# Prologue of an adaptive feed-forward kernel on one core: the adapters' split, the variances' norm and the value product take other places around tile 0

## The chip, the cores and the metric

The kernel runs on one core of one Trainium2 chip. The metric is the device time of one execution in microseconds (us), the median of several runs. A core has five engines that run their own instruction streams and wait for each other with semaphores: TensorE (PE: matmuls, with its weight loads shown apart as PEld), VectorE (DVE), ScalarE (ACT), GpSimd (POOL) and SyncE (SP), which here issues nearly all DMAs.

## The reference

The input x holds 128 samples of 64 channels by 1024 values. Cut to what matters:

```python
def layer0(x):                        # cond: one 64x64 matrix per sample, picked from 16
    h = einsum('bct,bcd->bdt', x, W0[itok_B_0_15])
    query = h @ Wq.T                                        # 64 wide
    scores = (query @ Wr.T) @ (aux_keys @ Wr.T).T / sqrt(48) + log_rel     # 256 slots
    top 8 of scores -> softmax(query . key / 8 + log_rel) -> weighted sum of aux_values
    aux_out = that @ Wvd.T @ Wvu.T
    log_var = log1p(var(h)); norm_var = log_var / (mean(log_var) + 1e-6)   # mean over all rows
    learned = gelu(h @ Wu1.T + bu1) @ Wu2.T + bu2
    gate = sigmoid(.5 * clip((clip(.5*norm_var + 2.5*sigmoid(learned), 0, 5) - .5) / 1.5, 0, 1) - 1)
    return h + gate * aux_out         # gate under 0.05 is 0
def layer1(x):                        # cond: base weight plus a rank-16 adapter, one of 32 per sample
    y = x @ base_weight.T + base_bias + (x @ A[ids].T) @ B[ids].T
    return y @ W_base.T + b_base + fourier_update(y)        # linear in y
x = x + layer0(x);  x = x + layer1(x)
```

All of the second layer is linear, so the kernel folds it into one 1024x1024 matrix M and one constant row. `norm_var` needs the mean over all 8192 rows before any tile can be gated.

## The kernel before, in words

The 128 samples form 64 tiles of two samples: 128 rows by 1024 columns. The program has three stages, whose parts for each engine run one after the other on it.

- `setup_stage` and `fold_stage` build M (`m32`, eight chunks of 128x1024) and the adapters' right side, and compute every tile's row variances beside it.
- `main_stage` has a prologue and then `step(n, p)` for n = 0 to 64. Step n takes tile n through its first products and finishes tile n - 1. Step 0 stands alone in the code and carries prologue work beside it; the steps behind it run in a loop of two steps a turn. Within each engine the order of instructions is exactly the order in which the code is written; nothing is rescheduled.

Matmuls in high precision are split in a high and a low part and done as three products (`product3`, lines 81 to 85). The low part of M, `m16_lo`, is made one chunk at a time on DVE by `m_low(k)` (line 1402) from `m32` and the high part that ACT made in `m_high(k)`.

Step 0 on each engine, as far as the change touches it:

- PE: tile 0's first product with 24 matmuls (lines 83 to 85), then the product with the picked matrices (line 1323), for which it waits for `pa_lo` from DVE (line 1535). Then the mean of the variances (line 1331) and the big product with M, eight chunks of six matmuls (line 1346). Chunk k waits for `m_low(k)` (line 1338). Between chunks stand, behind chunk 1, a transposition of the query (line 1355, waits for `wa_ready`, because it overwrites the bank in which the adapters' product lies); behind chunk 3 the router's scores (lines 1367 and 1368, which wait for the transposed query and for `norm_ready`, since they overwrite the bank of the mean); behind chunk 5 `value_operand()` (line 1253, waits for `vb_ready`, since it overwrites the bank that `v_low` reads); behind chunk 6 the transpositions of the softmax weights (line 1375, wait for `exp_ready`). At the end PE waits for `vd_ready` (line 1380).
- DVE: prologue work up to `gates` (line 1475), `m_low(1)`, `m_low(2)`, then step 0 with `pa_lo` (line 1535), the query's two halves (lines 1541, 1543) and `z` (line 1545). Then `beside_first()`: `m_low(3)`, the adapters' split `wa_split` (lines 1489, 1490), `m_low(4)` to `m_low(7)`, `v_low` twice (line 1482, the low part of the value projection, two copies), the four small instructions of the norm (lines 1499 to 1502). After it the rest of the step: `arg` (line 1551), MAX8 (line 1555) on the scores and the top-8 chain, softmax and gate down to `scale` (line 1597), and the copy `vd` (line 1601).
- ACT: step 0's part, among it `m_high(4)` to `m_high(7)`, the copy `rhs_a` of the value projection (line 1109), the splitting of x for tile 1, the exponential (line 1147).
- POOL: the low parts of x for tile 1: `a_raw` (line 1178), `xt_lo` (line 1179), `x16_lo` (line 1184).
- SP: stores `wa_split` to memory (line 1000) after `wa_ready`, then waits for that store and for `vb_ready`, and loads the adapters of tiles 0 and 1 (lines 942 and 950; eight DMAs a tile), which the end of step 1 needs (line 1290).

Of the kernel before, what the change touches and what calls it, by code (L numbers as in the profile page):

```python
# [37 lines left out]
ALU = mybir.AluOpType  # L38
# [6 lines left out]
KC = HID // P  # L45
HALF = HID // 2
NCOND = 16
NLORA, RANK = 32, 16
# [22 lines left out]
def f(ap):  # L71

    return ap.bitcast(F32)
# [7 lines left out]
def product3(pe, out, a_hi, a_lo, b_hi, b_lo, start, stop, skip=False):  # L81

    pe.matmul(out, a_hi, b_hi, start=start, stop=False, skip_group_check=skip)  # L83
    pe.matmul(out, a_hi, b_lo, start=False, stop=False, skip_group_check=skip)  # L84
    return pe.matmul(out, a_lo, b_hi, start=False, stop=stop, skip_group_check=skip)  # L85
# [10 lines left out]
def known_positive(count):  # L96

    return not isinstance(count, int) or count > 0
# [676 lines left out]
def main_stage(nc, t, g, v, f_, pair, sem, tile, st):  # L775
# [88 lines left out]
    misc_ps = pair[3][:, HALF:HID]  # L864
# [6 lines left out]
    wa_split = b["pm_lo"][:].rearrange("p (l s r) -> p l s r", s=2, r=RANK)  # L871
# [21 lines left out]
    s = {n: sem("m_" + n) for n in names}  # L893
# [142 lines left out]
    def has_new(n):  # L1036
        return not isinstance(n, int) or n < NT

    def has_old(n):
        return not isinstance(n, int) or n > 0  # L1040

    def arrived(n, p, each):

        return (n - p) * (each // 2) + each
# [152 lines left out]
    def tensor(pe):  # L1197
# [49 lines left out]
        def value_operand():  # L1247

            pe.wait_ge(s["av_in"], 32)
            pe.wait_ge(s["vb_ready"], 1)  # L1250
            for c in range(2):
                for k in range(KC):
                    last = pe.matmul(out_ps[:, c * BOT:(c + 1) * BOT], av_t[:, k, c * P:(c + 1) * P],
                                     b["wvd_t"][:, k, :], start=(k == 0), stop=(k == KC - 1))
            last.then_inc(s["vd_mm_done"], 1)
# [4 lines left out]
        def step(n, p):  # L1260
# [56 lines left out]
            if has_new(n):  # L1317

                pe.wait_ge(loaded["bd"][p], arrived(n, p, BPT))
                pe.wait_ge(s["pa_lo_ready"], n + 1)  # L1320
                if known_positive(n):
                    pe.wait_ge(s["z_ready"], n)
                product3(pe, mix_ps[:, 0:HQW], b["bd"][:, p, 0, :], b["bd"][:, p, 1, :],
                         b["pa_hi"][:, p, HQ[p]], b["pa_lo"][:, p, HQ[p]],
                         True, True).then_inc(s["mixq_done"], 1)
                if known_positive(n):
                    pe.wait_ge(s["pm_lo1_ready"], n)
                if not has_old(n):
                    pe.wait_ge(s["lsum1_ready"], 1)
                    pe.wait_ge(s["router_split"], 2)  # L1330
                    pe.matmul(score_ps[:, 0:1], g["ones"][:], b["mean"][:, 0:1], start=True, stop=True
                              ).then_inc(s["mean_done"], 1)
                    pe.wait_ge(s["const_placed"], 17)
                pe.wait_ge(s["x16_lo_ready"], n + 1)
                for k in range(KC):
                    if not has_old(n):
                        pe.wait_ge(s["m16_hi_ready"], k + 1)
                        pe.wait_ge(s["m16_lo_ready"], k + 1)
                    x_h = b["x16_hi"][:, p, k * P:(k + 1) * P]
                    x_l = b["x16_lo"][:, p, k * P:(k + 1) * P]  # L1340
                    first, end = k == 0, k == KC - 1
                    for lhs, m, a, z in ((x_h, m16_hi, first, False), (x_h, m16_lo, False, False),
                                         (x_l, m16_hi, False, end)):
                        for h in range(2):
                            c = slice(h * HALF, (h + 1) * HALF)
                            last = pe.matmul(pm_ps[:, c], lhs, m[:, k, c], start=a, stop=z)  # L1346
                    if end:
                        last.then_inc(s["s1b_done"], 1)
                    if k == (0 if has_old(n) else 1):
                        pe.wait_ge(s["q_split"], n + 1)  # L1350
                        if not has_old(n):
                            pe.wait_ge(s["wa_ready"], 1)
                        if known_positive(n):
                            pe.wait_ge(s["hm_ready"], n)
                        pe.transpose(misc_ps[:, 0:P], f(b["query"][:]), g["ident"][:]
                                     ).then_inc(s["qt_done"], 1)
                    if k == (2 if has_old(n) else 3):

                        pe.wait_ge(s["qt_ready"], n + 1)
                        if not has_old(n):  # L1360
                            pe.wait_ge(s["norm_ready"], 1)
                        if known_positive(n):
                            pe.wait_ge(s["logits_ready"], n)
                        if not has_old(n):
                            pe.wait_ge(s["logrel_placed"], 64)
                            pe.wait_ge(s["router_split"], 2)
                        pe.matmul(score_ps, b["q_a"][:], b["router_a"][:], start=True, stop=False)  # L1367
                        pe.matmul(score_ps, b["q_b"][0:BOT + 2, :], b["router_b"][0:BOT + 2, :],  # L1368
                                  start=False, stop=True).then_inc(s["score_done"], 1)
                    if k == 5 and not has_old(n):  # L1370
                        value_operand()
                    if k == 6:
                        pe.wait_ge(s["exp_ready"], n + 1)
                        for c in range(2):
                            last = pe.transpose(misc_ps[:, (c + 1) * P:(c + 2) * P],  # L1375
                                                b["probs"][:, c * P:(c + 1) * P], g["ident"][:])
                        last.then_inc(s["et_done"], 1)

                if not has_old(n):
                    pe.wait_ge(s["vd_ready"], 1)  # L1380

        steps(pe, step)

    def vector(dve):
# [3 lines left out]
        def link(ins):  # L1388

            chain[0] += 1  # L1390
            ins.then_inc(s["m_chain"], 1)
            dve.wait_ge(s["m_chain"], chain[0])
# [7 lines left out]
        def m_low(k):  # L1400
            dve.wait_ge(s["m16_hi_ready"], k + 1)
            dve.scalar_tensor_tensor(m16_lo[:, k, :], m32[:, k, :], M_SCALE, m16_hi[:, k, :],
                                     ALU.mult, ALU.subtract).then_inc(s["m16_lo_ready"], 1)
# [71 lines left out]
        dve.tensor_scalar(b["gates"][:, 3:6], b["gates"][:, 0:3], 0.5, None, ALU.mult  # L1475
                          ).then_inc(s["gates_ready"], 1)

        m_low(1)
        m_low(2)

        def v_low(p):
            return dve.tensor_tensor(b["rhs_b"][0:BOT, p, :], out_ps[0:BOT, :], f(b["rhs_a"][0:BOT, :]), ALU.subtract)

        def beside_first():

            m_low(3)
            dve.wait_ge(s["wa_mm_done"], KC // 2)
            wa3 = misc_ps.rearrange("p (l r) -> p l r", r=RANK)
            link(dve.tensor_copy(wa_split[:, :, 0, :], wa3))
            dve.tensor_tensor(wa_split[:, :, 1, :], wa3, f(wa_split[:, :, 0, :]), ALU.subtract  # L1490
                              ).then_inc(s["wa_ready"], 1)
            for k in range(4, KC):
                dve.wait_ge(s["v_mm_ready"], 1)
                m_low(k)
            dve.wait_ge(s["va_ready"], 1)
            v_low(0)
            v_low(1).then_inc(s["vb_ready"], 1)
            dve.wait_ge(s["mean_done"], 1)
            link(dve.tensor_scalar(b["mean"][:, 1:2], score_ps[:, 0:1], 1.0 / (NT * P), 1e-6, ALU.mult, ALU.add))
            link(dve.reciprocal(b["mean"][:, 2:3], b["mean"][:, 1:2]))  # L1500
            link(dve.tensor_scalar(b["lv_num"][:], b["lv_log"][:], b["mean"][:, 2:3], 0.5, ALU.mult, ALU.mult))
            dve.tensor_scalar(g["norm_var"][:], b["lv_num"][:], 1.25, None, ALU.add
                              ).then_inc(s["norm_ready"], 1)

        def step(n, p):
            if has_old(n):
# [26 lines left out]
            if has_new(n):  # L1533
# [13 lines left out]
                if not has_old(n):  # L1547
                    beside_first()
# [146 lines left out]
```

## Time and profile before

| what | value |
|---|---|
| median of 3 runs | 1592.76 us (1592.39 to 1595.8) |
| profiled execution, its own time | 1595.65 us |
| its span, first to last instruction | 1593.8 us |
| PE busy | 1549.6 us, 97% of the span |
| DVE, ACT, POOL busy | 55%, 52%, 32% |
| chain that ended last, by engine | PE 85%, POOL 6%, issue 5% |
| PE, longest wait in the stretch from 300 to 345 us | 9.3 us, in front of line 1367 |

Times in the rows are microseconds from the span's start, unless marked ns. A row of the timeline gives start, duration, engine, line, operation, output and inputs; in brackets stands how long the engine had been idle before it, and what released it. "issue" as a releaser means that the profile found no instruction whose end fits. Consecutive instructions of one engine overlap a little, since one starts while the last drains, so the distance of two starts is what an instruction costs its queue.

### The profile page before, as it was taken

What the parts mean: (1) busy time and instruction counts of PE and PEld (TensorE: products, weight loads), DVE (VectorE), ACT (ScalarE), POOL (GpSimd) and SP (SyncE); (2) the same over time, 40 slices, a digit from 0 to 9 for tenths busy, and PEclk for the clock granted to TensorE, in tenths of its full rate; (3) what the DMA queues carried; (4) which work ended last, traced back from release to release, by engine and by line L of the source; (5) the groups of instructions that cost most, each with busy time, mean ns of one, the idle gap of its engine ahead of it and who ended that gap; (6) DMA issues with size and microseconds to landing.
All of it is one profiled execution on the core that took longest, in us unless ns stands there. A gap on an engine that the chain in (4) does not pass through costs nothing.

```text
span 1593.8 us, 27390 instructions
## 1 busy us (share of the span) xinstructions
PE 1549.6 (97%) x7676; PEld 1046.5 (66%) x7676; DVE 868.8 (55%) x2526; ACT 822.3 (52%) x1595; POOL 503.8 (32%) x274
## 2 busy tenths in 40 slices
PE   7899999979999999999999999999999999999998
PEld 2577777646666666666666666666666666666665
DVE  4666777864455555555554455544555445544553
ACT  4565666545544454555554554454555555455542
POOL 3665666322222222222222222222222222222220
PEclk9899999989999999999999999999999999999999
DMA  9567665522322322333323332322222223223221
GB/s 340 174 225 224 187 181 161 173 66 89 87 87 89 89 89 88 90 91 95 91 87 90 95 92 88 87 87 87 87 87 87 87 87 87 88 89 88 87 72 50
DMA packets 160293, 176.49 MB, mean 111 GB/s; under 512 B 104656, under 2 KB 123043, under 8 KB 160142
## 3 DMA queue, kind: packets, MB, share of 16 engines
q1 hardware_dynamic: 157062, 165.75, 34.5%
q10 hardware_dynamic: 3208, 10.48, 1.9%
q8 instruction: 9, 0.15, 0.0%
q14 instruction: 14, 0.11, 0.0%
HBM read 136.49 MB, written 39.32 MB: 110 GB/s over the span
## 4 chain that ended last, share of the span: by engine, by line
PE 85%; POOL 6%; issue 5%; DVE 2%; ACT 1%; DMA 1%; POOLq 0%; ACTq 0%; SPq 0%; DVEq 0%
PE pair L1346 42%; PE pair L83 8%; PE pair L85 7%; PE pair L84 7%; PE pair L1307 6%; POOL v_lo L237 6%; PE pair L1315 6%; PE pair L1281 2%; PE pair L439 1%; PE pair L1368 1%; PE pair L1367 1%; PE pair L1375 1%; PE pair L1208 1%; PE pair L1296 1%; DMA fourier<-in_fourier 1%
## 5 line engine op out<-in xcount | busy, mean ns | idle before, releaser
L1178 POOL TENSOR_TENSOR t_narrow<-t_a_raw,t_narrow 128x256 fp32r<-128x256 f32 x64 | 47.1, 736 | 900.3 <-ACT t_xt_hi L1057 900.3
L1346 PE MATMUL pair<-m_hi,t_x_hi 128*128 128x512 f16 x1024 | 306.8, 381 | 0.0
L1346 PE MATMUL pair<-m_lo,t_x_hi 128*128 128x512 f16 x1024 | 305.5, 380 | 0.0
L1346 PE MATMUL pair<-m_hi,t_x_lo 128*128 128x512 f16 x1024 | 304.9, 379 | 0.0
L1551 DVE SCALAR_TENSOR_TENSOR t_arg<-t_z 128x256 f32<-128x256 f32 x64 | 133.5, 2086 | 145.3 <-ACT t_z L1141 145.3
L83 PE MATMUL pair<-t_narrow,t_xt_hi 128*128 128x352 f32 x512 | 191.0, 373 | 0.0
L237 POOL TENSOR_TENSOR v_lo<-v_x,v_hi 128x1024 fp32r<-128x1024 f32 x64 | 154.3, 2413 | 97.9 <-ACT v_hi L231 97.9
L1346 PEld LDWEIGHTS pair<-m_hi,t_x_lo 128*128 128x128 f16 x1024 | 100.4, 98 | 121.5 <-issue 1.1
L1346 PEld LDWEIGHTS pair<-m_lo,t_x_hi 128*128 128x128 f16 x1024 | 100.4, 98 | 121.4 <-issue 1.1
L85 PE MATMUL pair<-t_narrow,t_xt_lo 128*128 128x352 f32 x512 | 168.2, 329 | 0.0
L84 PE MATMUL pair<-t_narrow,t_xt_hi 128*128 128x352 f32 x512 | 168.2, 329 | 0.0
L1179 POOL TENSOR_TENSOR t_xt_lo<-t_xt,t_xt_hi 128x1024 fp32r<-128x1024 f32 x64 | 151.6, 2368 | 0.0
L1346 PEld LDWEIGHTS pair<-m_hi,t_x_hi 128*128 128x128 f16 x1024 | 90.1, 98 | 90.9 <-issue 18.2
L1184 POOL TENSOR_TENSOR t_x_lo<-t_xt,t_x_hi 128x1024 f16<-128x1024 f32 x64 | 137.4, 2146 | 28.1 <-ACT t_x_hi L1062 28.1
L1508 DVE SCALAR_TENSOR_TENSOR t_pm_lo<-pair,t_unscale,t_pm_hi 128x512 fp32r<-128x512 f32 x64 | 48.1, 751 | 120.3 <-ACT t_pm_hi L1114 120.3
L83 PEld LDWEIGHTS pair<-t_narrow,t_xt_hi 128*128 128x128 f32 x512 | 96.9, 189 | 9.1
L1144 ACT ACTIVATE t_th<-t_arg 128x256 f32<-128x256 f32 x64 | 26.6, 416 | 146.2 <-DVE t_arg L1551 146.2
L84 PEld LDWEIGHTS pair<-t_narrow,t_xt_hi 128*128 128x128 f32 x512 | 97.0, 189 | 1.7
L85 PEld LDWEIGHTS pair<-t_narrow,t_xt_lo 128*128 128x128 f32 x512 | 96.8, 189 | 0.0
L228 ACT ACTIVATE squares<-v_x 128x1024 bf16<-128x1024 f32 x64 | 67.5, 1054 | 54.2 <-DVE blk_lo L726 38.0
L1525 DVE TENSOR_TENSOR t_hm<-pair,lora_mask 32x128 f32<-32x128 f32 x64 | 17.9, 279 | 135.4 <-PE pair L1296 135.4
L1307 PE MATMUL pair<-t_pm_hi,t_bd 128*128 128x512 f32 x256 | 87.2, 422 | 0.0
(241 smaller groups left out, 2985.9 us busy)
## 6 DMA issues: line engine op xcount, KB each, us to landing
v_x<-in_x SPq DMA_DIRECT2D x64, 512.0 KB, 3.5
t_xt<-in_x_t SPq DMA_DIRECT2D x64, 512.0 KB, 3.2
out<-t_out_sb SPq DMA_DIRECT2D x64, 512.0 KB, 2.7
t_rhs_b<-bk_hi SPq DMA_DIRECT2D x256, 64.0 KB, 2.3
t_a_raw<-in_lora_a SPq DMA_DIRECT2D x128, 64.0 KB, 2.9
t_bd<-w_kinds SPq DMA_DIRECT2D x128, 64.0 KB, 2.2
t_rhs_c<-bk_lo SPq DMA_DIRECT2D x128, 64.0 KB, 2.2
blk_raw<-in_left_blocks ACTq DMA_DIRECT2D x10, 512.0 KB, 4.4
```

Of the source, the lines that this page charges most:

```text
L83: pe.matmul(out, a_hi, b_hi, start=start, stop=False, skip_group_check=skip)
L84: pe.matmul(out, a_hi, b_lo, start=False, stop=False, skip_group_check=skip)
L85: return pe.matmul(out, a_lo, b_hi, start=False, stop=stop, skip_group_check=skip)
L228: act.activation(v["squares"][:, s, :], v["v_x"][:, slot, :], ACT.Square, accum_out=g["x_sq"][:, bass.ds(n, 1)])
L237: pool.tensor_tensor(v["v_lo"][:, s, :], v["v_x"][:, slot, :], f(v["v_hi"][:, s, :]), ALU.subtract).then_inc(v["v_lo_ready"], 1)
L1179: pool.tensor_tensor(b["xt_lo"][:], b["xt"][:, p, :], f(b["xt_hi"][:]), ALU.subtract).then_inc(s["xlo_ready"], 1)
L1184: pool.tensor_tensor(b["x16_lo"][:, p, :], b["xt"][:, p, :], b["x16_hi"][:, p, :], ALU.subtract).then_inc(s["x16_lo_ready"], 1)
L1307: pe.matmul(out_ps[:, c], lhs, b[rhs][:, c], start=start, stop=False)
L1315: last = pe.matmul(out_ps[:, c], lhs, rhs[:, c], start=False, stop=end)
L1346: last = pe.matmul(pm_ps[:, c], lhs, m[:, k, c], start=a, stop=z)
L1508: dve.scalar_tensor_tensor(b["pm_lo"][:, 0:HALF], pm_ps[:, 0:HALF], unscale(n - 1), f(b["pm_hi"][:, 0:HALF]), ALU.mult, ALU.subtract)
L1551: dve.scalar_tensor_tensor(b["arg"][:], b["z2"][:], 1.0, b["z"][:], ALU.add, ALU.mult).then_inc(s["arg_ready"], 1)
```

## The change

Three things take another place; no instruction is added, removed or changed in size.

- The adapters' split (DVE) goes from behind `m_low(3)` in `beside_first()` to the place in front of step 0 where `m_low(1)` and `m_low(2)` stood; these go to the head of `beside_first()`.
- The norm of the variances (DVE) goes from behind `v_low` to a place in front of `m_low(3)`; `m_low(7)` goes behind `v_low`. The wait for `v_mm_ready`, the end of the value projection on PE, goes; the wait for `va_ready` (ACT's copy of that projection) stands in front of `m_low(6)`.
- The value product (PE) goes from behind chunk 5 of the product with M to behind chunk 6, in front of the transpositions of the softmax weights.

```diff
-                    if k == 5 and not has_old(n):
+                    if k == KC - 2 and not has_old(n):
                         value_operand()
@@ vector(), in front of step 0
-        m_low(1)
-        m_low(2)
+        dve.wait_ge(s["wa_mm_done"], KC // 2)
+        wa3 = misc_ps.rearrange("p (l r) -> p l r", r=RANK)
+        link(dve.tensor_copy(wa_split[:, :, 0, :], wa3))
+        dve.tensor_tensor(wa_split[:, :, 1, :], wa3, f(wa_split[:, :, 0, :]), ALU.subtract
+                          ).then_inc(s["wa_ready"], 1)
@@ beside_first()
-            m_low(3)
-            dve.wait_ge(s["wa_mm_done"], KC // 2)
-            wa3 = misc_ps.rearrange("p (l r) -> p l r", r=RANK)
-            link(dve.tensor_copy(wa_split[:, :, 0, :], wa3))
-            dve.tensor_tensor(wa_split[:, :, 1, :], wa3, f(wa_split[:, :, 0, :]), ALU.subtract
-                              ).then_inc(s["wa_ready"], 1)
-            for k in range(4, KC):
-                dve.wait_ge(s["v_mm_ready"], 1)
-                m_low(k)
-            dve.wait_ge(s["va_ready"], 1)
-            v_low(0)
-            v_low(1).then_inc(s["vb_ready"], 1)
+            m_low(1)
+            m_low(2)
             dve.wait_ge(s["mean_done"], 1)
             link(dve.tensor_scalar(b["mean"][:, 1:2], score_ps[:, 0:1], 1.0 / (NT * P), 1e-6, ALU.mult, ALU.add))
...
             dve.tensor_scalar(g["norm_var"][:], b["lv_num"][:], 1.25, None, ALU.add
                               ).then_inc(s["norm_ready"], 1)
+            for k in range(3, KC - 2):
+                m_low(k)
+            dve.wait_ge(s["va_ready"], 1)
+            m_low(KC - 2)
+            v_low(0)
+            v_low(1).then_inc(s["vb_ready"], 1)
+            m_low(KC - 1)
```

What this makes of the instruction streams. On DVE, around the first instructions of step 0 (`t_pm_lo<-pair` are the two instructions of the adapters' split, L1402 is `m_low`, L1535 is `pa_lo`); - is before, + is now:

```order
 L1475 TENSOR_SCALAR t_gates<-t_gates 128x3
-L1402 SCALAR_TENSOR_TENSOR m_lo<-m,t_scale,m_hi 128x1024 x2
+L1480 CAST t_pm_lo<-pair 128x32x16
+L1481 TENSOR_TENSOR t_pm_lo<-pair,t_pm_lo 128x32x16
 L1535 SCALAR_TENSOR_TENSOR t_pa_lo<-pair,t_x_unscale,t_pa_hi 128x352
 L1541 CAST t_query<-pair 128x64
 L1543 TENSOR_TENSOR t_query<-pair,t_query 128x64
 L1545 TENSOR_TENSOR t_z<-pair,t_bu 128x256
+L1402 SCALAR_TENSOR_TENSOR m_lo<-m,t_scale,m_hi 128x1024 x2
```

Two instructions of 1024 elements a row in front of `pa_lo` give place to two of 512.

On DVE behind `z`, in the kernel before (`t_rhs_b` is `v_low`, `t_mean` to `norm_var` the norm):

```order
L1402 SCALAR_TENSOR_TENSOR m_lo<-m,t_scale,m_hi 128x1024
L1489 CAST t_pm_lo<-pair 128x32x16
L1490 TENSOR_TENSOR t_pm_lo<-pair,t_pm_lo 128x32x16
L1402 SCALAR_TENSOR_TENSOR m_lo<-m,t_scale,m_hi 128x1024 x4
L1482 TENSOR_TENSOR t_rhs_b<-pair,t_rhs_a 64x1024 x2
L1499 TENSOR_SCALAR t_mean<-pair 128x1
L1500 RECIPROCAL t_mean<-t_mean 128x1
L1501 TENSOR_SCALAR t_lv_num<-t_lv_log,t_mean 128x64
L1502 TENSOR_SCALAR norm_var<-t_lv_num 128x64
L1551 SCALAR_TENSOR_TENSOR t_arg<-t_z 128x256
```

And the same place in the changed kernel:

```order
L1402 SCALAR_TENSOR_TENSOR m_lo<-m,t_scale,m_hi 128x1024 x2
L1492 TENSOR_SCALAR t_mean<-pair 128x1
L1493 RECIPROCAL t_mean<-t_mean 128x1
L1494 TENSOR_SCALAR t_lv_num<-t_lv_log,t_mean 128x64
L1495 TENSOR_SCALAR norm_var<-t_lv_num 128x64
L1402 SCALAR_TENSOR_TENSOR m_lo<-m,t_scale,m_hi 128x1024 x4
L1485 TENSOR_TENSOR t_rhs_b<-pair,t_rhs_a 64x1024 x2
L1402 SCALAR_TENSOR_TENSOR m_lo<-m,t_scale,m_hi 128x1024
L1551 SCALAR_TENSOR_TENSOR t_arg<-t_z 128x256
```

Two `m_low` stand ahead of the norm instead of five and two `v_low`; one `m_low` stands behind `v_low`.

On PE, the end of step 0's product with M (L1253 is the value product, L1375 the transposition of the softmax weights):

```order
+L1346 MATMUL pair<-m_hi,t_x_hi 128x512 x2
+L1346 MATMUL pair<-m_lo,t_x_hi 128x512 x2
+L1346 MATMUL pair<-m_hi,t_x_lo 128x512 x2
 L1253 MATMUL pair<-t_wvd_t,t_out_sb 128x64 x16
-L1346 MATMUL pair<-m_hi,t_x_hi 128x512 x2
-L1346 MATMUL pair<-m_lo,t_x_hi 128x512 x2
-L1346 MATMUL pair<-m_hi,t_x_lo 128x512 x2
 L1375 MATMUL pair<-ident,t_probs 128x128 x2
```

Chunk 6 of the product with M now stands ahead of the value product. The streams of ACT, POOL and SP are the same as before.

## Rows read from the trace of the kernel before

**Rows 1.** Waits from 300 to 345 us: who waited for whom, total, times, longest.

```profile
PE pair L1367 <- issue: 9.3, 1, 9.3
```

**Rows 2.** One step of the loop: busy time by engine, granted clock, DMA share.

```profile
367.60:387.20 19.60, 19.60 (x105) 13.03 (x103) 9.88 (x33) 9.88 (x21) 5.17 (x3) 1.00 0.30 89
```

**Rows 3.** Timeline of DVE in step 0: start, duration, line, operation, idle before.

```profile
317.26 2.46 DVE L1402 SCALAR_TENSOR_TENSOR m_lo<-m,t_scale,m_hi 128x1024 f16<-128x1024 f32 x2
319.65 0.57 DVE L1535 SCALAR_TENSOR_TENSOR t_pa_lo<-pair,t_x_unscale,t_pa_hi 128x352 fp32r<-128x352 f32 x1
321.54 0.23 DVE L1541 CAST t_query<-pair 128x64 fp32r<-128x64 f32 x1 [1.32 <-PE pair L85]
321.94 0.41 DVE L1545 TENSOR_TENSOR t_z<-pair,t_bu 128x256 f32<-128x256 f32 x1
...
323.47 0.68 DVE L1489 CAST t_pm_lo<-pair 128x512 fp32r<-128x512 f32 x1
...
324.79 9.28 DVE L1402 SCALAR_TENSOR_TENSOR m_lo<-m,t_scale,m_hi 128x1024 f16<-128x1024 f32 x4
334.00 2.34 DVE L1482 TENSOR_TENSOR t_rhs_b<-pair,t_rhs_a 64x1024 fp32r<-64x1024 f32 x2
336.26 0.14 DVE L1499 TENSOR_SCALAR t_mean<-pair 128x1 f32<-128x1 f32 x1
...
337.03 0.42 DVE L1551 SCALAR_TENSOR_TENSOR t_arg<-t_z 128x256 f32<-128x256 f32 x1
338.45 0.43 DVE L1555 MAX8 t_top<-pair 128x8 f32<-128x256 f32 x1 [1.00 <-PE pair L1368]
...
343.31 0.16 DVE L1597 TENSOR_TENSOR t_col<-t_col 128x1 f32<-128x1 f32 x1
```

**Rows 4.** Single `m_low` instructions: ns min/median/max, first and last start; two windows.

```profile
L1402 DVE SCALAR_TENSOR_TENSOR m_lo<-m,t_scale,m_hi x1: 1275/1275/1275, 322.3 to 322.3; 128x1024 f16<-128x1024 f32 x1
L1402 DVE SCALAR_TENSOR_TENSOR m_lo<-m,t_scale,m_hi x2: 3136/3246/3355, 327.7 to 330.9; 128x1024 f16<-128x1024 f32 x2
```

**Rows 5.** Timeline of POOL in step 0.

```profile
325.76 0.90 POOL L1178 TENSOR_TENSOR t_narrow<-t_a_raw,t_narrow 128x256 fp32r<-128x256 f32 x1 [9.11 <-ACT t_xt_hi L1057]
326.61 3.32 POOL L1179 TENSOR_TENSOR t_xt_lo<-t_xt,t_xt_hi 128x1024 fp32r<-128x1024 f32 x1
329.90 3.10 POOL L1184 TENSOR_TENSOR t_x_lo<-t_xt,t_x_hi 128x1024 f16<-128x1024 f32 x1
```

**Rows 6.** Timeline in step 1: one instruction of POOL, one of DVE.

```profile
357.03 2.36 POOL L1179 TENSOR_TENSOR t_xt_lo<-t_xt,t_xt_hi 128x1024 fp32r<-128x1024 f32 x1
```

```profile
357.22 0.41 DVE L1545 TENSOR_TENSOR t_z<-pair,t_bu 128x256 f32<-128x256 f32 x1
```

**Rows 7.** Timeline of ACT in step 0.

```profile
325.74 0.26 ACT L1136 CAST t_q_b<-pair 64x128 fp32r<-64x128 f32 x1
...
340.84 0.19 ACT L1147 ACTIVATION_READ_ACCUMULATOR t_probs<-t_logits,t_col 128x1 f32 x1
```

**Rows 8.** Timeline of PE at the end of step 0 and in step 1.

```profile
337.22 0.77 PE L1367 MATMUL pair<-t_router_a,t_q_a 128*128 128x512 f32 x1 [9.30 <-issue]
...
341.93 3.68 PE L1253 MATMUL pair<-t_wvd_t,t_out_sb 128*128 128x64 f32 x32
...
348.07 0.52 PE L83 MATMUL pair<-t_narrow,t_xt_hi 128*128 128x352 f32 x1
...
353.30 0.73 PE L1307 MATMUL pair<-t_pm_hi,t_bd 128*128 128x512 f32 x2
```

**Rows 9.** Short windows: columns as in Rows 2 (clock is third from the end).

```profile
331.00:337.20 6.20, 0.00 (x0) 0.01 (x1) 6.09 (x9) 0.00 (x0) 1.99 (x1) 0.50 0.00 0
...
340.20:341.20 1.00, 1.00 (x5) 0.45 (x4) 0.93 (x6) 0.60 (x2) 0.00 (x0) 0.86 0.50 131
```

**Rows 10.** SP's timeline: the last adapter load of tile 0.

```profile
342.76 0.37 SPq L950 DMA_DIRECT2D t_rhs_c<-bk_lo  x1
```

**Rows 11.** The page's DMA issues: operation, count, KB, us to landing.

```profile
t_rhs_c<-bk_lo SPq DMA_DIRECT2D x128, 64.0 KB, 2.2
```

## The prediction

> **What bounds the kernel now.** I read the waits around step 0 first, then a window over one step of the loop, then the timelines of PE, DVE, POOL, ACT and SP through step 0.
>
> In the loop PE is busy through the whole of a step, 19.60 us of 19.60 at a granted clock of 1.00 [rows 2]. The loop is PE's, and nothing of this change stands in it: a gain or a loss made before the loop is carried to the end unchanged. So the only question is when PE begins step 1. Before, that is 348.07, the first matmul of tile 1 [rows 8].
>
> In front of it PE stands idle for 9.3 us, the longest wait of the stretch [rows 1]. The releaser is called "issue", so it has to be found by times. The waiting instruction is the router's score at 337.22 [rows 8], which needs two things. The transposed query was ready at 326.00 (325.74 + 0.26) [rows 7]. The norm of the variances begins at 336.26 and `arg` behind it at 337.03 [rows 3]; the norm is complete about 0.1 later, and PE starts 0.2 after 337.03. So it is the norm that PE waits for, and the norm waits in no semaphore: it stands in DVE's queue behind `m_low` 3 to 7 and `v_low`. DVE is without a gap from 321.54 to 337.45 [rows 3]. After the wait two paths run to the end of step 0. PE has chunks 4 to 7, the value product and the transpositions, 337.22 to 348.07, with no further wait that the timeline shows. DVE has MAX8 at 338.45, released by PE's score, to `scale` at 343.31, then the copy `vd` (0.3). So PE's own work ends last, by 4 us, and it could not begin because of the norm.
>
> One more thing is to be seen on DVE. `m_low` alone takes 1.28 us, but two of them 3.36 and 3.14 [rows 4]. Both lie where POOL works: POOL's three subtractions run from 325.76 to 333.00, and the second and third start at 326.61 and 329.90 and take 3.32 and 3.10 [rows 5], where the same kind takes 2.36 in step 1 [rows 6]. The ends interlock: each engine's instruction finishes about 1.1 (DVE) or 2.1 to 2.3 (POOL) after the other's. They take turns. Four `m_low` so cost 9.28 [rows 3] and not 4 x 1.22 = 4.9.
>
> **The change part by part.** I rebuild DVE's stream with distances of starts from rows 3: one `m_low` 1.20, the split 1.32 (323.47 to 324.79), the norm 0.77 (336.26 to 337.03), one `v_low` 1.13 (334.00 to 336.26, halved).
>
> *Split ahead of `pa_lo`.* At 317.26 the adapters' product on PE is long finished, so the added wait costs nothing. Two `m_low` (317.26 to 319.65, 2.39) give place to the split (1.32): `pa_lo` starts at 318.6 instead of 319.65. It needs ACT's high half, which that row shows only as ready before 319.65; if that were as late as 319.65 the gain would be 0, and if it is earlier the gain is 1.07. I take 1.0. PE's small product and with it the query on DVE (a wait of 1.32 stays, since it is the same chain) come at 320.5 and `z` begins at 320.9. `wa_ready` comes at 318.6, so the transposition behind chunk 1 loses a possible wait. SP can store the split about 4 us sooner; its next wait but one is for `vb_ready`, so nothing stands behind that which could suffer.
>
> *`m_low(1)`, `m_low(2)` behind `z`.* They start at 321.2 and 322.4 and end at 323.7. PE's chunk 1 waits for the first; PE then starts chunks 1 and 2 a little later than it could, in a stretch where it had 9.3 us to spare. Cost nothing; it would cost at most 2.4, if nothing later held PE. That cover is not gone: chunks 4 to 7 hang on DVE too.
>
> *Norm in front of `m_low(3)`.* It needs PE's mean, one matmul behind the small product, ready about 320.7. The norm runs 323.6 to 324.4; `norm_ready` at 324.5 instead of 337.1. Now the transposed query (326.0) is what the scores wait for. Scores at about 326.2 to 327.5. The wait of 9.3 is gone as such, and what is late next is the low part of M, chunk by chunk.
>
> *The turns with POOL.* POOL's start hangs on ACT, whose stream does not move: 325.76. `m_low(3)` 324.4 to 325.6; `m_low(4)` to 326.8; POOL's first subtraction behind it, to 327.4; `m_low(5)` to 328.5; POOL's second to 330.7; `m_low(6)` to 331.8; POOL's third to 333.9. PE does chunks 3 to 6 behind them, chunk 6 from 331.9 to about 333.2.
>
> *`v_low` in front of `m_low(7)`.* Now the two `v_low` stand beside POOL's third subtraction, where before it was an `m_low`. Does `v_low` take turns too? It reads one operand from PSUM, one from SBUF. The nearest row of this form is `z` in step 1: 0.41 at 357.22, wholly inside POOL's 357.03 to 359.39, and 0.41 in step 0 with POOL idle [rows 3, 6]. So it costs the same beside POOL. Bounds: 0 extra, or the wait until POOL ends, 333.9 - 331.8 = 2.1. I take 0 by that row. `v_low` 331.8 to 334.1 (`vb_ready`), `m_low(7)` to 335.3 (POOL is done by then), `arg` starts at 335.3.
>
> The Trainium skill (SBUF — State Buffer, Who interferes with whom) says that a DVE instruction with two SBUF inputs and a GpSimd instruction that reads SBUF block each other fully, and one with at most one SBUF input outside the two-port modes does not. The turns of `m_low`, whose inputs both lie in SBUF, agree with it (3.36 against 1.28). Its words also give the order of issue as what decides who blocks; by that rule alone the sum would be what stands above, and by a reading in which any DVE instruction blocks it would be 2.1 longer.
>
> *DVE's end.* MAX8 starts 0.4 behind `arg`, at 335.7, with the scores there since 327.5: the wait of 1.00 is gone. MAX8 to `scale` was 343.31 - 338.45 = 4.86: `scale` at 340.6, `vd` copied by 340.9. The exponential's end moves likewise, from 341.03 [rows 7] by 2.75 to 338.3. In all DVE's end of the chain comes 2.75 earlier: 1.0 of MAX8's wait, 1.0 from the split, and the rest from the third POOL instruction, which no `m_low` waits out any longer (less what rounding takes).
>
> *Value product behind chunk 6.* PE can start it at `vb_ready`, 334.2. It takes 3.68 at full clock [rows 8]: to 337.9. Then the transpositions wait for the exponential, 338.3. Behind the value product stood chunks 6 and 7 and the transpositions, 348.07 - 345.61 = 2.46; of these chunk 6 is gone ahead, so (2.46 - 0.2) / 2 + 0.2 = 1.3 is left: PE is through at 339.7. It waits for `vd`, and begins step 1 at 341.0. So PE's own work no longer ends last; DVE's gate chain does, by 1.3.
>
> **Sum.** 341.0 - 348.07 = -7.1 us. With 0.3 for a clock that is not full everywhere (next part) I forecast -6.8. The profiled execution has 1593.8 of span in 1595.65, so it would be about 1588.9. It lay 2.9 above the median of the runs, 1592.76; from the median the forecast is **1586.0 us**.
>
> *Who else could be late in step 1.* The adapters of tile 0. Their last load was issued 342.76 + 0.37 [rows 10] after `vb_ready` at 336.34, and lands 2.2 later [rows 11]: 9.0 behind `vb_ready`. Now 334.1 + 9.0 = 343.1. They are needed just ahead of line 1307, which is 353.30 - 348.07 = 5.2 behind the start of the step [rows 8]: 346.2. There are 3 us to spare.
>
> **The rivals.**
>
> *A, PE's clock is low at the value product.* Before, the granted clock was 0.50 from 331.0 to 337.2 with PE idle, and rose at about 340.7, some 3.5 behind the resumed work [rows 9, 8]. This is the 1.2 GHz level. In the changed kernel PE has short gaps (about 2 before chunk 6, 1 before the value product) instead of one of 9.3. For a full clock speaks that no gap is as long; against it, that much of 329 to 334 is still idle. From 334.2 there are 3.68 + 1.3, about 5, of work and a wait for the exponential. With 3.5 of it at half speed PE is through at 334.2 + 3.5 + (5.0 - 1.75) = 341.0, just as DVE: gain 6.9 to 6.5. At half speed throughout: 344.2, gain 3.9, 1588.9.
>
> *B, `v_low` takes turns with POOL after all.* Then `vb_ready` 336.2, `m_low(7)` to 337.4, MAX8 at 337.8, `vd` at 343.0, step 1 at 343.1: gain 5.0, 1587.8. For it speaks only that `v_low` is long and was not seen beside POOL; against it the row of `z`.
>
> *C, the change gains little, because something else in step 1 holds it: the adapters.* If their loads came as late as 345.3 + 0, as before, they would still be in time; they would have to be delayed by 3 us over my sum before the first is lost, for instance by DMAs that now fall together. A delay of 7 would leave a gain of 3, 1590.
>
> *D, slower.* The clock falls in the broken-up stretch from 328 on and stays at 0.50 into the loop. Up to 344.2 it costs what A says; from there each us at full clock's work costs one more. The 3.9 that are left are used up when the low level lasts until 344.2 + 7.8 = 352.0; lasting to 356 it would be 1594.8. Against it: with work at hand the clock rose in about 3.5 before.
>
> **Chances.** My forecast with A's mild form 0.68; A at half speed throughout 0.07; B 0.12; C 0.05; D 0.03; 0.05 for a clock that is full from 320 on, whereby DVE's query comes 0.5 sooner and the gain is up to 7.6. The range: 1585.2 to 1586.3 for the forecast itself, to which comes the scatter of medians (1592.39 to 1595.8 in three runs of before, mostly upwards); with A and B taken in it is 1583.0 to 1590.0. A measurement of this kernel tells 0.2%, or 3.2 us, from no change. Faster by more than that: all but part of C and A, and D: 0.92. Within: 0.05. Slower: 0.03.
>
> **What would show it.** Right, step by step: `pa_lo` at 318.6; `norm_ready` before 325 and the scores by 326.5 with no wait of 9 us in front of them; the `m_low` behind `v_low` at 1.2 to 1.3 and each `v_low` at 1.2; POOL's third subtraction still near 3; MAX8 about 2.8 earlier with no wait for PE; a wait of PE for `vd` of about 1 at the start of step 1, and that start at about 341. Wrong: a `v_low` over 2 us (B); the value product at over 5 us (A); a wait in front of line 1295 or 1307 in step 1 (C); a granted clock under 1.00 behind 345 (D); or a start of step 1 at 341 with an unchanged time, which would mean that the loop gives back what comes before it.

## The result, and the profile after

| kernel | median us (runs) | ratio to before, 95% interval |
|---|---|---|
| before | 1592.76 | |
| changed | 1586.11 (5, 1581.14 to 1587.77) | 0.9949 [0.993, 0.9969] |
| changed, in a second series | 1588.26 (10) against 1592.08 (30) | 0.9972 [0.9956, 0.9988] |

The change makes the kernel faster, by 6.65 us in the first comparison and 3.8 in the second; neither interval contains 1, and the two overlap. Forecast were a gain of 6.8 and a median of 1586.0.

The profiled execution of the changed kernel (span 1579.3) is 14.5 us shorter than that of before. That is twice what the change does, and it has to be taken apart. As a first anchor take DVE's `gates` instruction (line 1475): 317.19 before, 312.94 after, so 4.25 was won ahead of anything that the change touches. The end is seen in the transposition of line 1286, once a tile (copies, ns min/median/max, first and last start); first of the kernel before, then of the changed one:

```profile
L1286 PEld LDWEIGHTS pair<-ident,t_u_sb x64: 138/141/143, 351.0 to 1582.5; 128*128 128x128 f32 x64
```

```profile
L1286 PEld LDWEIGHTS pair<-ident,t_u_sb x64: 139/141/142, 339.2 to 1570.8; 128*128 128x128 f32 x64
```

From first to last the loop takes 1231.5 and 1231.6: it neither adds nor returns anything. Behind the last one before needs 11.3, the changed kernel 8.5, and the short windows show why; before first (the third column from the end is the granted clock), an early stretch and the tail:

```profile
54.00:61.00 7.00, 7.00 (x18) 5.08 (x18) 3.56 (x7) 3.31 (x5) 3.32 (x3) 0.53 0.49 160
1582.50:1593.80 11.30, 6.62 (x18) 4.46 (x18) 1.65 (x5) 1.43 (x3) 0.00 (x0) 0.67 0.12 48
```

```profile
51.00:58.00 7.00, 5.50 (x22) 4.02 (x23) 3.47 (x7) 2.52 (x4) 5.02 (x3) 1.00 0.45 153
1570.70:1579.30 8.60, 3.89 (x18) 2.68 (x18) 1.68 (x6) 1.43 (x3) 0.00 (x0) 0.88 0.16 63
```

In both places the clock was lower in the profile of before. The other profiles, in which this code is the same, have it either way: from 54 to 61 us the clock is anything from 0.50 to 1.00, with and without the change, and behind the last transposition they need 8.5 to 11.3. So this is scatter and not the change. What is left is step 0: 30.88 from `gates` to the first matmul of step 1 before (317.19 to 348.07), 23.42 after (312.94 to 336.36). **7.5 us is what the change gives in these two profiles.**

DVE of the changed kernel, to be held against [rows 3]:

```profile
313.01 0.67 DVE L1480 CAST t_pm_lo<-pair 128x512 fp32r<-128x512 f32 x1
...
314.33 0.57 DVE L1535 SCALAR_TENSOR_TENSOR t_pa_lo<-pair,t_x_unscale,t_pa_hi 128x352 fp32r<-128x352 f32 x1
315.77 0.23 DVE L1541 CAST t_query<-pair 128x64 fp32r<-128x64 f32 x1 [0.86 <-PE pair L85]
...
318.89 0.15 DVE L1492 TENSOR_SCALAR t_mean<-pair 128x1 f32<-128x1 f32 x1
...
319.67 7.43 DVE L1402 SCALAR_TENSOR_TENSOR m_lo<-m,t_scale,m_hi 128x1024 f16<-128x1024 f32 x4
327.03 2.34 DVE L1485 TENSOR_TENSOR t_rhs_b<-pair,t_rhs_a 64x1024 fp32r<-64x1024 f32 x2
329.29 1.26 DVE L1402 SCALAR_TENSOR_TENSOR m_lo<-m,t_scale,m_hi 128x1024 f16<-128x1024 f32 x1
330.49 0.41 DVE L1551 SCALAR_TENSOR_TENSOR t_arg<-t_z 128x256 f32<-128x256 f32 x1
330.82 0.42 DVE L1555 MAX8 t_top<-pair 128x8 f32<-128x256 f32 x1
...
335.67 0.16 DVE L1597 TENSOR_TENSOR t_col<-t_col 128x1 f32<-128x1 f32 x1
```

The norm starts at 318.89, ahead of `m_low(3)`; the two `v_low` take 2.34 as before, the `m_low` behind them 1.26, and MAX8 has lost its wait. PE and POOL, against [rows 8] and [rows 5]:

```profile
327.25 0.59 PE L1346 MATMUL pair<-m_hi,t_x_hi 128*128 128x512 f16 x2 [1.63 <-DVE m_lo L1402]
...
329.51 3.76 PE L1253 MATMUL pair<-t_wvd_t,t_out_sb 128*128 128x64 f32 x32 [0.80 <-DVE t_rhs_b L1485]
...
336.36 0.43 PE L83 MATMUL pair<-t_narrow,t_xt_hi 128*128 128x352 f32 x1 [1.20 <-DVE vd L1601]
```

```profile
325.99 3.11 POOL L1184 TENSOR_TENSOR t_x_lo<-t_xt,t_x_hi 128x1024 f16<-128x1024 f32 x1
```

The single wait of 9.3 [rows 1] has become 1.6, 0.8 and 1.2 (and 0.8 and 0.3 earlier, in front of chunks 1 and 3), and the last, for `vd`, says that DVE's gate chain now ends step 0. SP issued the last adapter load of tile 0 at 334.87, and nothing in step 1 waited for it.

### The profile page after: what moved, and what is told of

Read it like the earlier page. It is cut to its first block, busy times and chain, and to the rows that moved or that the text cites. A ratio compares the mean times of both kernels' runs of the same rounds, so it can differ in the third digit from the quotient of the medians.

```text
span 1579.3 us, 27387 instructions
## 1 busy us (share of the span) xinstructions
PE 1541.1 (98%) x7676; PEld 1040.8 (66%) x7676; DVE 865.0 (55%) x2526; ACT 823.1 (52%) x1595; POOL 505.0 (32%) x274
## 4 chain that ended last, share of the span: by engine, by line
PE 82%; POOL 7%; issue 5%; DVE 3%; DMA 1%; ACT 1%; SPq 1%; ACTq 0%; POOLq 0%; DVEq 0%
PE pair L1346 41%; PE pair L83 7%; PE pair L85 7%; PE pair L84 7%; POOL v_lo L237 7%; PE pair L1307 6%; PE pair L1315 6%; PE pair L1281 2%; DMA v_x<-in_x 1%; PE pair L1368 1%; PE pair L1367 1%; PE pair L1208 1%; PE pair L1375 1%; DVE m_lo L1402 1%; PE pair L1296 1%
```

## The experiments

Since the whole time scatters by 5 us and more, each kernel was also read by two distances: D, from `gates` to the first matmul of step 1, and E, to the same matmul from the start of ACT's `pa_hi` (line 1123), which in every profile starts 0.12 to 0.13 behind the end of PE's first product. (ACT's queue also waits for `gates` ahead of it, at line 1100, but `gates` was never more than 0.03 later than that product.) Before: D 30.88, E 30.61. Changed: 23.42 and 23.14. Ratios are to before. Their intervals are 4 to 7 us wide and those of most kernels below overlap with that of the change, so what follows rests on the distances, from one profile of each kernel, and on their repeating in the changed kernel.

**The value product's move alone.** Before, with

```diff
-                    if k == 5 and not has_old(n):
+                    if k == KC - 2 and not has_old(n):
```

> The kernel before, with one part of the change: the value product on PE behind chunk 6. I measure D, from the start of DVE's gates instruction to the first matmul of step 1: 30.88 us before (317.19 to 348.07), 23.42 with the whole change (312.94 to 336.36). Theory (PE is held by the norm that stands late in DVE's queue, and the value product's place matters only once that wait is gone): the wait of 9.3 in front of the scores stays, and PE has the same work behind it, so D stays 30.9 within 0.3 and the time is that of before. Rival (the value product's place is itself worth something, because it blocked PE in front of chunk 6): D shorter by 1 to 2.

```profile
333.36 0.76 PE L1367 MATMUL pair<-t_router_a,t_q_a 128*128 128x512 f32 x1 [6.88 <-issue]
```

Ratio 0.9998 [0.9977, 1.0018]. The wait in front of the scores stayed, at 6.9. D was 30.08, E 27.64; why E is not 30.6 is told under "who is first" below, where a profile of the kernel before that is of the same kind has 27.69. The move alone gives nothing.

**The norm's move alone.** Before, with the norm's five lines in front of `m_low(3)`:

```diff
+            dve.wait_ge(s["mean_done"], 1)
...
             m_low(3)
```

> The kernel before, with the norm alone moved in front of m_low(3); split, m_low(7), v_low and value product stay. Theory (it is the order of DVE's whole queue that counts, and the next wait is the one for vb_ready): the scores start about 10 us sooner, without the 9.3 wait, but PE then waits 7 us in front of the value product until v_low is done at about 337.3 on before's scale (the same DVE work in another order). The clock falls in that wait, which costs about 1.75. Step 1 starts about 345.2 on that scale, D about 28.0, a gain of 2.9. Rival (the norm was the wait and its move is the whole gain): D about 23.4, a gain of 7.5.

D 30.86, E 30.60, ratio 0.9985 [0.9968, 1.0003]. PE's rows:

```profile
326.53 0.59 PE L1367 MATMUL pair<-t_router_a,t_q_a 128*128 128x512 f32 x1
...
334.85 7.06 PE L1253 MATMUL pair<-t_wvd_t,t_out_sb 128*128 128x64 f32 x32 [4.89 <-DVE t_rhs_b L1482]
```

The scores come 8 us sooner, and step 1 not at all: 4.89 of it is the new wait for `vb_ready`, and the value product takes 7.06 instead of 3.68, all of it at the low level. I had allowed 1.75 for the clock; it cost 3.4, and 1.3 more in chunk 6 (341.71 to 344.27 instead of 1.3), with the level back at 1.00 only from about 344.3, 9.4 behind the resumed work. The rival, in which the norm is the whole gain, falls.

**The changed kernel with the value product behind chunk 5.**

```diff
-                    if k == KC - 2 and not has_old(n):
+                    if k == 5 and not has_old(n):
```

> The changed kernel with the value product back behind chunk 5. Theory: with the full clock PE would do value product, chunk 6, transpositions and chunk 7 in 3.7 + 2.5 = 6.2 us from vb_ready (329.5 on the changed kernel's scale) to 335.7, just ahead of vd at 336.03, so the move would be worth nothing (D 23.4). But PE now stands idle for 4 us in front of it instead of 1.6 and 0.8; before, an idle stretch of 3.0 was followed by a clock of 0.50. With that, PE is through at 337.4 and D is about 24.6. Rival (chunk 6 in front of the value product is what makes the gain): D at 25 or more.

D 27.60, E 27.29, ratio 0.9981 [0.9961, 1.0001]. DVE is as in the changed kernel (MAX8 at 17.88 from `gates` in both), but

```profile
334.22 7.06 PE L1253 MATMUL pair<-t_wvd_t,t_out_sb 128*128 128x64 f32 x32 [3.62 <-DVE t_rhs_b L1485]
```

By the bare distances the rival came closer (27.60; theory 24.6). Whether it is the place or the clock is for the next kernel.

**The same, with PE kept busy.**

```diff
+                        pe.wait_ge(s["z_ready"], 1)
+                        for d in range(14):
+                            pe.matmul(mix_ps, x_h, m16_hi[:, k, 0:HALF], start=True, stop=True)
                         value_operand()
```

> The changed kernel with the value product back behind chunk 5, and in front of it 14 needless matmuls of 512 columns on PE (about 3.0 us at full clock, into a bank whose content is no longer wanted), so that PE hardly idles while it waits for v_low. They lie inside PE's idle time of 3.6. Theory (chunk 6 in front of the value product pays by keeping the clock, not by doing its work earlier): the value product takes 3.7 and D falls from 27.60 to 23.5. Rival (the place of chunk 6 as such, or the wait itself): D stays at 27 or rises.

```profile
331.03 3.19 PE L1373 MATMUL pair<-m_hi,t_x_hi 128*128 128x512 f16 x14
335.06 3.76 PE L1253 MATMUL pair<-t_wvd_t,t_out_sb 128*128 128x64 f32 x32 [0.85 <-DVE t_rhs_b L1488]
```

E 22.65 against 27.29, with more work on PE. (This execution was of the other kind, told below, which makes D, 26.63, useless; by E that kind is worth only 0.5 for the changed kernel.) A profile of the changed kernel of that kind, shown under "who is first", has 22.65 too: with the clock kept, the value product behind chunk 5 is as good as behind chunk 6, so its place is worth what it saves in clock. The time, 0.9979 [0.9961, 0.9998], could not be told from that without filler.

**The norm alone, with 20 such matmuls.**

> The kernel with the norm alone moved, plus 20 needless matmuls of 512 columns (4.3 us) in PE's idle time of 4.9 in front of the value product. Without them E was 30.60, as before, and the value product took 7.06. Theory (the norm's early place frees PE, and all of it is given back at half clock): the value product takes 3.7, chunk 6 and 7 run at full clock, and E falls to 26.5 to 27.2 if POOL is first (23.5 if DVE is first). Rival (the norm's move is worth nothing by itself since vb_ready is no earlier): E stays at 30 to 30.6.

E 28.94, ratio 0.9974 [0.9957, 0.9991]: between the two. The clock fell all the same, within the value product, with 1.22 of idle time ahead of it (two windows, clock third from the end):

```profile
337.70:339.00 1.30, 1.29 (x12) 1.30 (x12) 1.23 (x5) 0.42 (x1) 0.00 (x0) 1.00 0.00 0
340.00:342.60 2.60, 2.60 (x14) 2.60 (x14) 1.33 (x9) 1.35 (x5) 0.00 (x0) 0.50 0.35 82
```

The value product took 5.11, and chunks 6 and 7 began at the low level as well. So the filler does not settle what the norm alone would be worth at full clock.

**The changed kernel with `m_low(7)` in front of `v_low`.**

```diff
             m_low(KC - 2)
+            m_low(KC - 1)
             v_low(0)
             v_low(1).then_inc(s["vb_ready"], 1)
-            m_low(KC - 1)
```

> The changed kernel with m_low(7) back in front of the two v_low. Theory (m_low, with two operands in SBUF, takes turns with POOL's subtractions, v_low, with one in PSUM, does not): m_low(7) meets POOL's third subtraction and waits it out, about 3.1 us instead of 1.26, and everything behind it on DVE, MAX8 and scale with it, comes 1.9 later; D about 25.3. Rival (the turns do not depend on which instruction stands there, or POOL is slowed instead): MAX8 where it was, D 23.4.

```profile
326.16 10.50 DVE L1402 SCALAR_TENSOR_TENSOR m_lo<-m,t_scale,m_hi 128x1024 f16<-128x1024 f32 x5
```

The fifth `m_low` cost 10.50 - 7.43 = 3.07, and MAX8 came 1.97 later, as the turns say. D was 29.22, not 25.3: PE waited 3.87 and the value product took 7.06, which the expectation had left out. So this one `m_low` behind `v_low` instead of ahead of it is worth 5.8 of D, 2.0 on DVE and the rest in PE's wait and clock. Ratio 0.9991 [0.9975, 1.0007].

**POOL held back.** Changed kernel; POOL waits for `m_low(6)` ahead of its first subtraction for tile 1 and for the gate's sum ahead of the third.

```diff
+                if not has_old(n):
+                    pool.wait_ge(s["m16_lo_ready"], KC - 1)
                 split_x(n + 1, 1 - p)
+                if not has_old(n):
+                    pool.wait_ge(s["lsum_ready"], 1)
```

> The changed kernel in which POOL starts the first two subtractions for tile 1 only when m_low(6) is done, and the third only when the gate's sum is ready (lsum_ready), so that m_low(3) to m_low(6) meet nobody. Theory (turns): four m_low take 4.9 instead of 7.43; the second subtraction now meets m_low(7), which waits about 0.9; D about 21.8. Rival (m_low is slow there for another reason, such as ACT or DMAs): still 7.4 for the four, D 23.4 or more.

```profile
323.28 4.86 DVE L1406 SCALAR_TENSOR_TENSOR m_lo<-m,t_scale,m_hi 128x1024 f16<-128x1024 f32 x4
328.06 2.34 DVE L1489 TENSOR_TENSOR t_rhs_b<-pair,t_rhs_a 64x1024 fp32r<-64x1024 f32 x2
330.32 3.18 DVE L1406 SCALAR_TENSOR_TENSOR m_lo<-m,t_scale,m_hi 128x1024 f16<-128x1024 f32 x1
```

Four `m_low` without POOL take 4.86 instead of 7.43: the turns are the cause. But the last one meets POOL now and takes 3.18, a wait of 1.9 where 0.9 was expected; D is 22.88, not 21.8; E 22.61, ratio 0.9958 [0.9944, 0.9973], no clear gain over the change.

**The changed kernel once more.**

> The changed kernel once more, unaltered. D (DVE's gates to the first matmul of step 1) was 23.42 with the granted clock at 1.00 all through step 0. If the two short gaps of PE (1.6 and 0.8) never let the clock fall, D is 23.4 again within 0.5. If they sometimes do, the value product takes 7.06 as in the three kernels of the first series that idled 3.6 to 4.9 in front of it, and D is about 26 to 27.6.

D 23.41, E 23.14, full clock from 321.2 to the end of step 0, value product 3.76, wait for `vd` 1.19. From 319.0 to 321.2, in chunks 0 and 1, the clock stood at 0.50, and D is the same all the same: there DVE's queue is what counts. The profile repeats; the ratio is that of the table's last line.

**Who is first.** Some profiles differ ahead of the change. POOL's `x16_lo` for tile 0 (line 1184) and DVE's router split (line 1471) start at about the same time, both with all inputs in SBUF. In the changed kernel's second profile POOL was first, and DVE waited:

```profile
312.27 2.40 DVE L1471 TENSOR_TENSOR t_router_b<-t_gelu,t_router_a 64x256 fp32r<-64x256 f32 x1
...
314.94 0.15 DVE L1475 TENSOR_SCALAR t_gates<-t_gates 128x3 f32<-128x3 f32 x1
```

Of 11 profiles of kernels that leave this race open 8 are so (in 2 of them it is the second instruction of line 1471 that waits); in 3 (value product alone, filler, split back) DVE was first, line 1471 took 0.42, and `gates` came 2.4 to 4.0 ahead of `pa_hi` instead of 0.2 to 0.5. The 4.0, in the filler kernel, has a second cause: the clock was 0.50 for about 3 us of PE's work in front of `gates`, so that PE's first product came 1.6 later against `gates`, and the two engines did not meet at all. That explains e.g. E of 27.64 above. One line on POOL takes the race away:

```diff
         split_x(0, 0)
+        pool.wait_ge(s["gates_ready"], 1)
         narrow_x(0, 0)
```

In the kernel before:

> The kernel before, in which POOL's subtraction for tile 0 (x16_lo) waits for DVE's gates. The traces so far fall in two kinds. Where POOL's subtraction started ahead of DVE's router instruction (line 1471), that instruction took 2.3 instead of 0.42, and gates came 0.3 before ACT's pa_hi; where DVE was first, gates came 2.4 before it. I measure E, from the start of ACT's pa_hi to the first matmul of step 1: before 30.61 (POOL first), the value-product-only kernel, whose DVE stream is the same, 27.64 (DVE first). The wait makes DVE always first. Theory: E about 27.6 and the time 3 us below before. Rival (the two kinds have nothing to do with the turn at line 1471): gates still at -0.3 in some profile, time as before.

E 27.69, as expected. The time moved by less than 3: 1592.07 against 1592.52, 0.9994 [0.9979, 1.0009]. In the changed kernel:

> The changed kernel with the same wait of POOL for gates. With DVE first, the split ahead of pa_lo leaves DVE idle (3.1 in the filler kernel, which ran that way), because ACT's pa_hi is not there yet, and m_low(1) and m_low(2) stand behind it. Theory: E about 22.6 against 27.6 for before with the same wait, so the change gains only 5.0 where DVE is first, against 7.5 where POOL is first. Rival: the gain is the same in both, E about 20.2.

E 22.65, ratio 0.9956 [0.9941, 0.997]. By E the change gives 7.5 where POOL is first and 5.0 where DVE is. (This profile had the 3 us of low clock ahead of `gates` too, 0.50 from 308 to 310, so POOL was held by ACT's `x_hi` and not by its new wait; E starts behind that.) DVE's rows say why:

```profile
310.77 0.15 DVE L1476 TENSOR_SCALAR t_gates<-t_gates 128x3 f32<-128x3 f32 x1
...
315.36 0.58 DVE L1536 SCALAR_TENSOR_TENSOR t_pa_lo<-pair,t_x_unscale,t_pa_hi 128x352 fp32r<-128x352 f32 x1 [3.11 <-ACT t_pa_hi L1123]
...
320.71 7.45 DVE L1403 SCALAR_TENSOR_TENSOR m_lo<-m,t_scale,m_hi 128x1024 f16<-128x1024 f32 x4
```

`pa_lo` cannot start before ACT's half, so the two `m_low` that were taken away in front of it had been free, and now stand behind `z`.

**The split's place**, first in the changed kernel, then with the forced order as well:

```diff
-        dve.wait_ge(s["wa_mm_done"], KC // 2)
-        wa3 = misc_ps.rearrange("p (l r) -> p l r", r=RANK)
...
+        m_low(1)
+        m_low(2)
@@ beside_first()
-            m_low(1)
-            m_low(2)
+            dve.wait_ge(s["wa_mm_done"], KC // 2)
+            wa3 = misc_ps.rearrange("p (l r) -> p l r", r=RANK)
...
             dve.wait_ge(s["mean_done"], 1)
```

> The changed kernel with the adapters' split behind z again (in front of the norm) and m_low(1) and m_low(2) in front of pa_lo. Prediction's reading: the split's place is worth 1.0 of DVE's chain, so MAX8 comes 1.0 later, D 24.4. Rival, formed from the comparison of the two traces: pa_lo and the query come 1.07 later, but DVE does the same work before MAX8 and its idle wait for the query is the same, so what is late at pa_lo is made good by the work that no longer stands behind z; MAX8 and D unchanged, 23.4 (23.9 if the longer wait for pa_lo lets PE's clock fall for the small product).

This profile had DVE first: D 22.83, E 20.41, so it can't be held against 23.14. Ratio 0.9967 [0.9954, 0.9979]; median 1584.97.

> The changed kernel with the split behind z and m_low(1), m_low(2) ahead of pa_lo, and POOL's wait for gates. Theory: the two m_low fill DVE's idle time in front of pa_lo, E 20.4 as in the profile of the split-back kernel that fell on the DVE-first kind, 2.2 below the changed kernel with the same wait; by time about 2.7 below the changed kernel and 10 below a profile of before with POOL first, in the median 8 to 9 below. Rival (the split's place is worth 1.0 the other way, as the prediction had it): E over 22.6.

```profile
315.50 0.15 DVE L1476 TENSOR_SCALAR t_gates<-t_gates 128x3 f32<-128x3 f32 x1
...
318.49 0.58 DVE L1536 SCALAR_TENSOR_TENSOR t_pa_lo<-pair,t_x_unscale,t_pa_hi 128x352 fp32r<-128x352 f32 x1 [0.46 <-ACT t_pa_hi L1123]
...
322.77 5.35 DVE L1403 SCALAR_TENSOR_TENSOR m_lo<-m,t_scale,m_hi 128x1024 f16<-128x1024 f32 x4
...
332.81 1.23 DVE L1561 TENSOR_SCALAR t_penalty<-t_rest 128x256 f32<-128x256 f32 x1
```

E 20.42, median 1582.75 (7 runs), ratio 0.9941 [0.9919, 0.9964]: the lowest median of all. By E it beats the changed kernel by 2.2 with the same order, 2.7 without; by time its interval overlaps with both. Only 1.1 of it is the filled idle time (two `m_low`, 2.4, in front of `pa_lo` instead of the split, 1.3). MAX8 comes 3.2 sooner behind `pa_hi` (13.94 against 17.11), because the four `m_low` also meet POOL once less, 5.35 against 7.45; then line 1561 takes 1.23 instead of 0.29 beside POOL's third subtraction, which gives 0.9 back.

## Why the prediction was right, point by point

The forecast of -6.8 is next to the first measured difference (-6.65) and 3.0 beyond the second (-3.8), whose interval reaches to -7.0; by the profiles the change gives 7.5 or 5.0, by who is first. The mechanism and its size stand on the profile distances: the sum put D at 341.0 - 317.19 = 23.8, measured were 23.42 and 23.41. That the first median was met within 0.15 is luck. The medians do not even rank the kinds: with POOL's wait in both kernels they differ by 1592.07 - 1584.16 = 7.9, where E says 5.0. And I summed only the kind in which POOL is first, not knowing of another; the profiles of before and after were both of that kind.

- *What bounds the kernel.* Right. The norm stood behind DVE's queue: moved alone it frees the scores by 8 us. The loop carries the gain unchanged (1231.5 and 1231.6).
- *Turns with POOL.* Right in size: four `m_low` 7.43 (summed: 7.4); 4.86 without POOL; `m_low(7)` 1.26 behind `v_low` and 3.07 ahead of it; `v_low` 1.2 each beside POOL's third subtraction. Rival B falls.
- *DVE's end.* Right within 0.6: MAX8 17.88 behind `gates`, summed 335.7 - 317.2 = 18.5. PE's small product ran at full clock, and the query's wait was 0.86 instead of 1.32; that is the case to which I had given 0.05. The 0.3 that I took off for the clock was not lost: -7.1 was the better number.
- *"1.0 from the split".* Wrong, though the positions in my sum did not use it. `pa_lo` came 1.07 sooner, but the same DVE work lies ahead of MAX8 in either order. By rows: MAX8 gained 3.38, of which 1.0 is its own wait, 1.9 the turn that `m_low(7)` lost (3.14 to 1.26) and 0.46 the query's wait. Nothing is left for the split. This is worked out from rows where POOL is first; in both profiles with the split back DVE was first. Where DVE is first, its new place costs 2.2 (E 22.65 against 20.42).
- *Value product behind chunk 6.* The order of the ends was right (PE waits 1.2 for `vd`, summed 1.3), the worth was not seen. At full clock I counted chunk 6 out of a stretch that would have fitted anyway. In the run it is 27.29 - 23.14 = 4.15 of the gain, because PE's idle stretch is filled and the clock stays. Rival A at half speed throughout left a gain of 3.9; with the value product behind chunk 5 30.61 - 27.29 = 3.3 is left. Its mild form, in which the clock is back 3.5 behind the resumed work and costs 1.75, was mis-sized: with the norm alone that took 9.4 and cost 4.6. The changed kernel escaped it in all three profiles (value product 3.76 in each); whether it does in every run is open.
- *Adapters (C) and slower (D).* Neither was seen.
- *Not foreseen:* the race at line 1471, which decides whether the change gives 7.5 or 5.0. How often each side wins in the unprofiled runs is open. The forced kernel before should have been 2 to 3 faster if POOL mostly won, and was 0.5 in the medians, with an interval from 3.3 faster to 1.4 slower.

## What to carry to other kernels

A wait that an in-order queue causes shows no semaphore of its own: look at what stands in front of the producer. Removing it alone can be worth nothing by the profile (here 30.60 against 30.61; the ratio of that run, 0.9985 [0.9968, 1.0003], does not tell it from a small gain), when the next wait lies in the same queue and the idle engine's clock falls; ask what fills the engine until the next wait ends. Where two engines reach for SBUF at the same moment, order them by a semaphore, or the comparison of two kernels is one of two races.

## What was not expected of the hardware

- The value product, 32 matmuls with 64 columns, ran at the 1.2 GHz level from end to end (7.06) behind idle stretches of 3.62, 3.87 and 4.89, although PE was busy throughout; behind 0.80 and 0.85 it took 3.76. In the norm-alone kernel with filler, behind 1.22, the clock stood at 1.00 until 339.8 and at 0.50 from 340.0, so it fell a little over 2 into the product. Before the change, with 512-column matmuls first, the clock was 0.50 from 340.0 to 340.4 and 0.91 from 340.4 to 340.8, so the level rose about 3.3 behind the resumed work.
- The turns are not symmetric for `v_low`: it was not held up by a subtraction of POOL that had started first (1.20), but in the kernel with POOL held back POOL's first subtraction, issued 0.16 behind a `v_low`, took 1.72 instead of 0.73. The Trainium skill (SBUF — State Buffer, Who interferes with whom) has it that a DVE instruction with at most one SBUF input, outside the two-port modes, does not contend with GpSimd; the 1.20 agree, this row does not:

```profile
328.22 1.72 POOL L1178 TENSOR_TENSOR t_narrow<-t_a_raw,t_narrow 128x256 fp32r<-128x256 f32 x1 [12.21 <-DVE m_lo L1406]
```

One row; its cause was not tested.
